# One fused product for q, k and v, one exponential for both heads, and biases carried in shifted weights

## The reference, cut to what matters

```python
ln  = layernorm(layernorm(x)) * g + b          # 4 x 512 x 128
xn  = layernorm(ctx) * g2 + b2                 # 4 x 77 x 96
q   = ln @ Wq.T
k,v = split(concat([xn @ Wkv.T, ln @ Wlkv.T])) # 77 + 512 keys
qn, kn = rmsnorm(q) * scale, rmsnorm(k)        # per head, 2 heads of 64
attn = softmax(where(mask, qn @ kn.T, -max))
x   = x + (attn @ v) @ Wo.T + bo
y   = layernorm(x)
g   = softmax(y @ Wg + bg); top 2 of 8 experts
x   = x + sum over the two of g[e] * (y @ W[e] + b[e])
```

## Time and profile before

| what | us |
|---|---|
| median of 3 timed runs | 128.02 (126.82 to 130.88) |
| span of the profiled execution, first to last instruction | 123.7 |
| median less span (launch and end, and the difference between executions) | 4.3 |
| busy: PE / DVE / POOL / ACT | 106.9 / 97.5 / 91.0 / 76.6 |

### The profile page before, as it was taken

How to read it: one execution, slowest core, us unless ns; L and a number is a source line. 1 busy time by engine, 2 the same in 40 slices (tenths; PEclk the granted TensorE clock), 3 DMA queues, 4 the chain that set the end, 5 groups by cost and what they waited for, 6 DMA issues and landing times. The chain is left out here.

```text
span 123.7 us, 2493 instructions
## 1 busy us (share of the span) xinstructions
PE 106.9 (86%) x683; PEld 69.0 (56%) x683; DVE 97.5 (79%) x376; ACT 76.6 (62%) x177; POOL 91.0 (74%) x117
## 2 busy tenths in 40 slices
PE   0579969999999999999999899999999998589800
PEld 0366957565844763358535356464678885357500
DVE  0746899699598295766988999999899979599780
ACT  1444748784668781985846646797549484843730
POOL 5544699977985789974877191276979998868893
PEclk9999985999999999999999999999999999976995
DMA  4514540000000000000000000000010011101111
GB/s 122 119 22 130 168 169 0 5 0 0 0 3 0 5 0 0 0 0 5 0 5 0 0 0 5 0 0 5 0 42 3 3 42 42 38 10 42 42 42 42
DMA packets 5971, 3.44 MB, mean 28 GB/s; under 512 B 2407, under 2 KB 5575, under 8 KB 5959
## 3 DMA queue, kind: packets, MB, share of 16 engines
q1 hardware_dynamic: 5127, 2.93, 8.0%
q10 hardware_dynamic: 832, 0.36, 1.1%
HBM read 2.24 MB, written 1.05 MB: 27 GB/s over the span
## 5 line engine op out<-in xcount | busy, mean ns | idle before, releaser
L588 ACT ACTIVATE probs<-PS,shift,rk 128x512 f32<-128x512 f32 (+1 forms) x40 | 25.5, 691 | 9.6 <-PE PS L1077 9.3
L635 ACT ACTIVATE scaled<-PS,w 128x128 f32<-128x128 f32 x64 | 18.4, 375 | 9.7 <-PE PS L947 7.0
L1098 PE MATMUL PS<-probs,V_sb 128*64 128x512 f32 (+1 forms) x80 | 18.2, 532 | 0.0
L420 POOL TENSOR_TENSOR esum<-probs,probs 128x1024 f32<-128x1024 f32 (+1 forms) x5 | 10.7, 2147 | 7.2 <-ACT probs L588 7.2
L945 PE MATMUL PS<-WeH,l2H 128*128 128x512 f32 x32 | 14.3, 446 | 0.5 <-ACT scaled L635 0.5
L470 POOL TENSOR_TENSOR pair<-scaled 128x256 f32<-128x256 f32 x16 | 12.0, 751 | 2.8 <-ACT scaled L635 1.5
L946 PE MATMUL PS<-WeL,l2H 128*128 128x512 f32 x32 | 13.3, 414 | 0.0
L947 PE MATMUL PS<-WeH,l2L 128*128 128x512 f32 x32 | 13.1, 410 | 0.0
L429 POOL TENSOR_TENSOR e<-probs,probs 128x1024 f32<-128x1024 f32 (+1 forms) x5 | 9.7, 1936 | 2.6 <-ACT probs L588 2.6
L1077 PE MATMUL PS<-QH,KH 64*128 64x512 f32 (+1 forms) x40 | 9.5, 463 | 0.4 <-DVE QL L766 0.4
L719 DVE TENSOR_SCALAR xh<-x_sb,mv,rstd 128x128 f32<-128x128 f32 x16 | 8.1, 566 | 2.0 <-POOL rstd L388 2.0
(11 more groups left out here) (149 smaller groups left out, 271.3 us busy)
## 6 DMA issues: line engine op xcount, KB each, us to landing
out_dram<-x2b SPq DMA_DIRECT2D x7, 128.0 KB, 1.7
x_sb<-in_x_dram SPq DMA_DIRECT2D x3, 256.0 KB, 3.4
We_sb<-in_L_ffn_W_dram SPq DMA_DIRECT2D x1, 512.0 KB, 5.2
x_sb<-in_x_dram SPq DMA_DIRECT2D x2, 128.0 KB, 2.4
bias_raw<-in_L_ffn_b_dram SPq DMA_DIRECT2D x12, 4.0 KB
Wlkv_sb<-in_L_xattn_Wlkv_dram ACTq DMA_DIRECT2D x1, 128.0 KB, 2.8
out_dram<-x2b SPq DMA_DIRECT2D x2, 64.0 KB, 1.6
ctx_sb<-in_ctx_dram SPq DMA_DIRECT2D x1, 115.5 KB
```

The lines of the kernel that those rows point to most:

```text
L420: pool.tensor_tensor(esum[p % 2][:, :, s], probs[p % 2][0][:, :, s], probs[p % 2][1][:, :, s], ALU.add).then_inc(e01_made, 1)
L588: act.activation(probs[p % 2][n][:, h, s], ps[:, s], ACT.Exp, bias=shift[:, 0:1], scale=rk[:, b, n, h:h + 1]).then_inc(probs_made, 1)
L635: last = act.activation(scaled[m % 2][:, e], ps[:, e], ACT.Copy, scale=w[:, m, e:e + 1])
L1098: last = pe.matmul(bank("value", p, 0)[h * D:(h + 1) * D, s], v, pr, start=(n == 0), stop=(n == KT - 1))
```

## The change

- FRONT has eight units of two tiles, REAR four whole batches. The tables are written anew, and waits count jobs by their place in them.
- `qkv`: one product of 384 columns for a token tile, tokens on the partitions for q, k and v. k goes q's way: one square, one reduce, one power (`rq`, now 8 columns for two tiles), one multiplication (`qkn`), four transposes for two tiles (`qkT`), a split of both. `ssk`, `msk` and `rk` are gone, and the ctx keys go the same way (`ckv`, `ckn`, `ckT`).
- `exp`: one instruction for both heads (two banks, 1024 columns), no scale from a tile, and scores of a tile end in one semaphore.
- `den`: three sources are multiplied by ones and accumulated (e01, e23, ctx), instead of DVE's two additions.
- The layernorm's last channel is replaced by 1, the last row of Wg and of the expert weights by the bias, and that row is subtracted from the others first (the channels of a layernorm sum to zero). `w3`, `gateT`, `wT`, `bias`, `x2b` and the addition of bg are gone; the subtraction (`weS`) and the rest WeL are made on POOL, WeH on ACT.
- The gate is three rounded products of 16 columns for a tile; only l2H is evicted by ACT, and l2L is made by DVE from PSUM.
- `pair`, `low` and `res` take two tiles at once, one store for each pair of tiles.

```diff
 CHOSEN = 3e38
 
 
-FRONT = ((0, 0, 2), (0, 2, 4), (1, 0, 4), (2, 0, 4), (3, 0, 4))
-REAR = ((0, 0, 4), (1, 0, 4), (2, 0, 4), (3, 0, 2), (3, 2, 4))
-
+FRONT = tuple((b, a, a + 2) for b in range(4) for a in (0, 2))
+REAR = ((0, 0, 4), (1, 0, 4), (2, 0, 4), (3, 0, 4))
+JOINED = (0, 1, 2, 3)
 
...
+            sp.dma_start(x_sb[:, 1], xv[1]).then_inc(x_in[1], 16)
             sp.dma_start(gq_b[:], row(qng).to_broadcast([P, D])).then_inc(gains_in, 16)
             sp.dma_start(gk_b[:], row(kng).to_broadcast([P, D])).then_inc(gains_in, 16)
-            sp.dma_start(x_sb[:, 1], xv[1]).then_inc(x_in[1], 16)
             sp.dma_start(mask8[:], mask).then_inc(mask_in, 16)
-            sp.dma_start(bo_b[:], row(bo).to_broadcast([P, C])).then_inc(bias_in, 16)
-            sp.dma_start(bg_b[:], row(bg).to_broadcast([P, E])).then_inc(bias_in, 16)
-            sp.dma_start(Wg_sb[:], Wg).then_inc(Wg_in, 16)
-            sp.dma_start(We_sb[:], We.rearrange("e h o -> h e o")).then_inc(We_in, 16)
-            sp.wait_ge(blk_zeroed, 1)
-            for t in range(T):
-                for k in range(3):
-                    r = k * T * E + E * t
-                    sp.dma_start(bias_raw[r:r + E, t], be).then_inc(blk_in, 16)
             for b in range(2, B):
                 sp.dma_start(x_sb[:, b], xv[b]).then_inc(x_in[b], 16)
+            sp.dma_start(bo_b[:], row(bo).to_broadcast([P, C])).then_inc(bo_in, 16)
+            sp.dma_start(Wg_sb[:], Wg[0:P - 1]).then_inc(Wg_in, 16)
+            sp.dma_start(Wg_last[:], Wg[P - 1:P].to_broadcast([P - 1, E])).then_inc(Wg_in, 16)
+            sp.wait_ge(Wg_zeroed, 2)
+            sp.dma_start(WgS[P - 1:P, 0:E], row(bg)).then_inc(bg_in, 16)
+            sp.dma_start(We_sb[0:P - 1], We[:, 0:P - 1].rearrange("e h o -> h e o")).then_inc(We_in, 16)
+            sp.dma_start(We_last[:], We[:, P - 1:P].rearrange("e h o -> h e o").to_broadcast([P - 1, E, C])).then_inc(We_in, 16)
+            sp.dma_start(We_sb[P - 1:P], be.rearrange("(a e) o -> a e o", a=1)).then_inc(We_in, 16)
 
...
                 step(pool.tensor_scalar(msq[:, b, a:e], ssq[:, b, a:e], 1.0 / D, RMS_EPS * RMS_EPS, ALU.mult, ALU.max))
-                pool.tensor_tensor(rq[:, b, a:e], msq[:, b, a:e],
...
-                pool.tensor_tensor(rk[:, b, a:e], msk[:, b, a:e],
-                                   half[:, 0:H * (e - a)].rearrange("p (t h) -> p t h", h=H), ALU.pow).then_inc(rk_made, 1)
+                pool.tensor_tensor(rqk[:, b, a:e], msq[:, b, a:e],
+                                   half[:, 0:2 * H * (e - a)].rearrange("p (t h) -> p t h", h=2 * H), ALU.pow).then_inc(rqk_made, 1)
...
+            def weS_(p, n):
+
+                pool.wait_ge(We_in, 48)
+                pool.tensor_tensor(We_sb[0:P - 1], We_sb[0:P - 1], We_last[:], ALU.subtract).then_inc(WeS_made, 1)
+
+            def weL_(p, n):
+
+                pool.wait_ge(WeH_made, 1)
+                pool.tensor_tensor(WeL[:], We_sb[:], WeH[:].bitcast(F32), ALU.subtract).then_inc(WeL_made, 1)
...
+            def sq_(p, n):
+                b, a, e = FRONT[p]
+                act.wait_ge(qkv_done, after("pe", "qkv", p))
+                if p >= 2:
+                    act.wait_ge(ssq_made, after("dve", "ssq", p - 2))
+                act.activation(qksq[:, p % 2], both("qkv", p, 0)[:, :, 0:2 * C], ACT.Square).then_inc(qksq_made, 1)
...
+                act.activation(QH[:, b % 2, a * P:e * P], bank("qkT", p, 0)[:, 0:(e - a) * P], ACT.Copy, scale=gain[:, 0:1])
+                act.copy(KH[:, b % 2, a * P:e * P], bank("qkT", p, 0)[:, (e - a) * P:2 * (e - a) * P]).then_inc(qkH_made, 1)
...
+            def weH_(p, n):
+                act.wait_ge(WeS_made, 1)
+                act.wait_ge(We_in, 48)
+                act.copy(WeH[:], We_sb[:]).then_inc(WeH_made, 1)
...
+                ps = both("score", p, n)
                 if n < T:
-                    act.wait_ge(rk_made, through(FRONT, b, n + 1))
+                    act.activation(probs[p % 2][n][:], ps[:], ACT.Exp, bias=shift[:, 0:1], scale=1.0).then_inc(probs_made, 1)
...
-            def ctx_ms_(p, n):
-                dve.wait_ge(css_done, 1)
-                dve.tensor_scalar(cms[:], bank("ctx_ss", 0, 0)[0:M, 0:B * H].rearrange("m (b h) -> m b h", h=H),
-                                  1.0 / D, RMS_EPS * RMS_EPS, ALU.mult, ALU.max).then_inc(cms_made, 1)
-
-            def esum1_(p, n):
-
-                s = slice(0, (REAR[p][2] - REAR[p][1]) * P)
-                dve.wait_ge(e01_made, p + 1)
-                dve.wait_ge(e23_made, p + 1)
-                step(dve.tensor_tensor(esum[p % 2][:, :, s], esum[p % 2][:, :, s], e23[:, :, s], ALU.add))
-
-            def esum2_(p, n):
-
-                s = slice(0, (REAR[p][2] - REAR[p][1]) * P)
-                dve.wait_ge(dve_step, count[0])
-                dve.wait_ge(probs_made, H * KT * (p + 1))
-                dve.tensor_tensor(esum[p % 2][0:M, :, s], esum[p % 2][0:M, :, s], probs[p % 2][T][0:M, :, s],
-                                  ALU.add).then_inc(esum_made, 1)
+            def ctx_ss_(p, n):
...
-            def w3_(p, n):
-
-                b, a, e = REAR[p]
-                s = slice(b * T + a, b * T + e)
...
-                dve.tensor_copy(w3[:, 0, 0:e - a], w[:, s])
-                dve.wait_ge(dve_step, step(dve.tensor_copy(w3[:, 2, 0:e - a], w[:, s])))
-                dve.tensor_tensor(w3[:, 1, 0:e - a], w[:, s], w3[:, 2, 0:e - a].bitcast(F32),
-                                  ALU.subtract).then_inc(w3_made, 1)
-
-            def wT_(p, n):
-                dve.wait_ge(gateT_done, p + 1)
-                if p >= 1:
-                    dve.wait_ge(bias_done, p)
-                dve.tensor_copy(wT[0:3 * T * E], bank("gateT", p, 0)[0:3 * T * E, 0:P]).then_inc(wT_made, 1)
-
-            def x2b_(p, n):
-
-                b, a, e = REAR[p]
-                dve.wait_ge(bias_done, p + 1)
-                dve.tensor_tensor(x2b[:, b, a:e].rearrange("p t c -> p (t c)"), bank("bias", p, 0)[:, 0:(e - a) * C],
-                                  x2[:, b, a:e].rearrange("p t c -> p (t c)"), ALU.add).then_inc(x2b_made, 1)
...
-            def ssk_(p, n):
-                b, a, e = FRONT[p]
-                free("ssk", p, 0)
-                pe.wait_ge(k_made, p + 1)
-                pe.wait_ge(consts_made, 2)
-                for t in range(a, e):
-                    last = pe.matmul(bank("ssk", p, 0)[:, (t - a) * H:(t - a + 1) * H], ksq[:, b % 2, t * P:(t + 1) * P],
-                                     heads[:], start=True, stop=True)
...
+                    last = pe.matmul(both("qkv", p, 0)[:, t - a, 0:3 * C], lnT[:, b % 2, t * P:(t + 1) * P], WT[:],
+                                     start=True, stop=True)
+                last.then_inc(qkv_done, 1)
...
+                for s in range(2):
+                    for t in range(a, e):
+                        k = s * (e - a) + t - a
+                        last = pe.transpose(bank("qkT", p, 0)[:, k * P:(k + 1) * P], qkn[:, p % 2, t - a, s * C:(s + 1) * C], ident[:])
+                last.then_inc(qkT_done, 1)
```

More of the change, by code:

```diff
@@ L241, in bank @@
+        pair = sb("pair", [P, 2, EH // 2, C])
+        low = [sb(f"low{n}", [P, 2, C]) for n in range(2)]
+        acc = [sb(f"acc{n}", [P, 2, C]) for n in range(2)]
+        part = [sb(f"part{n}", [P, 2, C]) for n in range(EH - 1)]
+        PS = [st.enter_context(nc.psum_tensor(f"PS{n}", [P, 2, S], F32)) for n in range(4)]
         def bank(kind, p, n, k=0):
-            return PS[banks[kind, p, n][k]]
+            number = banks[kind, p, n][k]
+            return PS[number // 2][:, number % 2]
@@ L641, in _ @@
+            for kind, p, n in JOBS["act"]:
+                does[kind](p, n)
         @block.vector
@@ L817, in x2_ @@
+                dve.wait_ge(denT_done, after("pe", "denT", b))
+                c = T // 2
+                sums = bank("denT", b, 0)[:, 0:c * P].rearrange("p (c h g k) -> p c h g k", c=c, h=H, g=2)
+                for g in range(a // c, e // c):
+                    divided = step(dve.reciprocal(rden[:, b, g * c:(g + 1) * c], sums[:, :, :, g, 0]))
+                dve.wait_ge(proj_done, after("pe", "proj", p))
                 dve.wait_ge(dve_step, divided)
@@ new lines, in sum_ @@
+                        if e < EH - 1:
+                            summed[i] = step(last)
+                last.then_inc(acc_made, 1)
+            does = dict(consts=consts_, gain=gain_, shift=shift_, mask=mask_, cbias=cbias_, wgsplit=wgsplit_, stats1=stats1_,
+                        apply1=apply1_, ssq=ssq_, qkn=qkn_, qkL=qkL_, ctx_stats=ctx_stats_, ctx_apply=ctx_apply_, ctx_ss=ctx_ss_,
+                        ckn=ckn_, ckL=ckL_, x2=x2_, stats2=stats2_, apply2=apply2_, l2L=l2L_, logits=logits_, mark=mark_,
+                        top=top_, sum=sum_)
@@ L935, in _ @@
+            for kind, p, n in JOBS["dve"]:
+                does[kind](p, n)
         @block.tensor
@@ L1180, in _ @@
```

(10 more changed lines are left out.)

893 lines of the change are left out of this document (390 added, 503 removed).

## The result

The changed kernel takes **159.83 us** (159.06 to 160.62, four runs), the kernel before 128.06 beside it: a ratio of 1.257, 95% interval 1.245 to 1.269. The prediction said 124.2, and its range ended at 129.0. The sign was wrong.

A forecast was written before the change was run, and what follows sets the result against it. PE was taken to set the pace to about 86 us, DVE and POOL to lead the 37.0 us end. 86.6 + 1.5 + 0.6 = 88.7, plus 31.2 gives 119.9 span, plus 4.3 gives 124.2 us; range 119.5 to 129.0.

The forecast's parts named there:

- The step that failed: Middle: the expert-weight subtraction and splits on POOL and ACT are covered; weights wait behind blanks, near 26 us; no cost.
- The slower rival: Later batches: powers in POOL's queue make PE wait 2.3 us before first scores of batches 1-3; 7 us, 131; chance 0.12.
- The front: Start up to the first score: keys now wait for the power, so first score at 20.0 in place of 17.5.
- The chain over the power: Front: batch 1 of x at 10.0, DVE statistics, POOL's two powers to 16.9, then unit 1's remaining steps to 20.0.
- The slow scores: After the first score: the same low-clock stretch again, 2.5 us later, at the same price of 0.43 a pass.
- The middle: First scores to batch 3's last value product: PE sets the pace, elementwise work stays covered; end at 88.7 against 86.6.
- Lag: At 24 us, PE is behind the kernel before by 1.5 us because of the later first score; between 0 and 3.
- PE's work: Removed and added PE jobs nearly cancel: +0.6 us, between -2 and +2; PE gains nothing.
- The paired banks: Middle: scores wait for one long exponential to free both banks, 0.2 each over 20 scores; 4 us, 128; chance 0.15.
- The end: After the last value product: DVE leads, 31.2 us in place of 37.0, saving 5.8.
- the held instructions: End: DVE's last-batch normalisation held once beside POOL's pairs, adding 3.6 us, giving 127.8; chance 0.08.
- From span to time: Whole kernel: median time kept 4.3 us above the profiled span, turning a span of 119.9 into 124.2.

The follow-up runs named there:

- e1_split: Changed kernel with its two large expert-weight loads each cut into loads of 112 and 15 partitions: 122.57 us, ratio to before 0.979.
- h1_122: As e1_split, but with the two loads cut at 122 partitions (122 and 5) in place of 112: 135.58 us, ratio 1.076.
- e4_before_127: Kernel before, with its one expert-weight load over 128 partitions written as loads of 127 and 1: 146.74 us, one run.
- e3_weS_late: Changed kernel with weS moved later in POOL's order and weH later in ScalarE's, loads unchanged: 140.35 us, one run.
- g1_pairs_wait: e1_split with POOL's batch 3 bias addition moved ahead of batch 1's power, and POOL's first batch 1 pair waiting for DVE's last normalisation: 120.41 us.

## Why the prediction was wrong, point by point

**The step that failed** is in the middle: "WeS, WeL and WeH go to POOL and ACT and are covered by the same work", with the expert weights "behind POOL's `blanks`" and "wanted by the first expert product". It looked at the subtractions and let the loads pass unpriced. Two things were left out. The load was not the old one: 128 partitions at 5.2 us from issue to landing had become two loads of 127 at 22 GB/s, 46 us (shown by e1_split, h1_122 and e4_before_127). They were issued at 31.5, too, and not near 26. And it is not the first expert product that wants the weights first: `weS` stands ahead of additions and powers in POOL's order, some 30 us sooner (e3_weS_late). For 35 us of standing and 2 at the lower clock the forecast had zero. I had asked of each engine's instruction what hides it, and of the DMAs only where they are issued. The slower rival, too, looked for a POOL queue that delays PE, but for its powers' length, not for a transfer in it.

**The rest of the sum** can be read off e1_split, whose stages are (front to the first score, middle to the last value product, end), and g1_pairs_wait's end:

```profile
0.00:19.80 19.80, 13.03 (x48) 7.58 (x48) 12.88 (x55) 8.78 (x20) 11.33 (x22) 1.00 0.30 84
19.80:86.90 67.10, 65.76 (x436) 33.25 (x440) 46.48 (x162) 39.14 (x63) 47.65 (x45) 1.00 0.08 17
86.90:120.40 33.50, 25.46 (x152) 19.46 (x152) 28.95 (x122) 18.77 (x67) 23.14 (x26) 0.97 0.10 32
```

```profile
87.10:118.70 31.60, 25.27 (x152) 19.53 (x152) 26.36 (x118) 18.77 (x67) 23.03 (x26) 0.95 0.10 34
```

- The front: first score at 19.80, forecast 20.0. The chain over the power came out, with two small errors against each other: batch 1 was there at 9.2 and not 10.0, and the steps behind the second power (done at 16.5, forecast 16.9) took 3.3 and not 2.9. But the chain did not hold PE alone: the ctx products, 1.9 us from 17.87 that no term of the forecast has there, end at 19.76, and PE goes from them to the score without a pause.
- The slow scores: forecast "the same stretch again". They did not come. From the first score on a pass of both heads takes 0.23 us at clock 1.00, where before it took 0.43. The kernel before had the lower level from 17.8 to 21.2, with PE busy throughout; 3.4 us at half the clock are 1.7 us too many, an estimate from these rows. Why the clock stays up in the new front was not tried.
- The middle: last value product done at 86.9, forecast 88.7. Lag and PE's work together came to +0.2 and not +2.1; by the estimate above most of that is the clock. Of the single prices, `den` of 24 instructions takes 1.44 (forecast 1.5 to 1.7) and a gate of twelve 1.3 (1.3).
- The paired banks: PE idles 1.34 us in the whole middle, and all of it ahead of one `denT` at 63.8, none ahead of a score (e1_split's trace). That rival is out; one exponential of both heads takes 1.11 (taken at 1.2).
- The end: 33.5, forecast 31.2. The missing 2.3 are the held instructions, the rival that I gave 0.08: 2.5 us on the four normalisations of batch 3. With them cured the end is 31.6. The same lies behind the long row of the first normalisation, and could be read in the trace of before: that instruction, the first of the four in DVE's row, starts at 23.05 and lasts 3.97 us, to 27.02; the second of two POOL instructions beside it is over at 26.93.

```profile
23.05 4.74 DVE L719 TENSOR_SCALAR xh<-x_sb,mv,rstd 128x128 f32<-128x128 f32 x4 [1.18 <-POOL rstd L388]
```

```profile
22.98 1.63 POOL L411 TENSOR_TENSOR crk<-cms,half 77x8 f32<-77x8 f32 x1
24.58 2.35 POOL L420 TENSOR_TENSOR esum<-probs,probs 128x1024 f32<-128x1024 f32 x1
```

- From span to time: 4.3 assumed. The profiled execution of e1_split has 122.14 for a span of 120.4, of the changed kernel 159.1 for 157.3: 1.8. The kernel before has 1.8 as well where both numbers are known (126.54 for 124.7, beside g1_pairs_wait). The distance had mixed a fast profiled execution with the median of others; with 1.8 the forecast span of 119.9 would have given 121.7.

So for the kernel without the slow loads the forecast span of 119.9 stands against 120.4: the middle's -1.8 and the end's +2.3 nearly cancel, which is luck and makes that sum look better than its terms.

## What to carry to other kernels

Ask of every load that a change touches into how many equal parts its partitions divide: one row more or less can turn a load of 5 us into one of 23, and here a cut into 112 and 15 mends it. Ask of every instruction that waits for a load not when its result is wanted, but what else is queued behind it and who wants that. And where a cheap elementwise instruction takes three times its usual time, look at what the neighbour engine does at that moment; a wait in the right place on the neighbour made it disappear.

## What was unexpected in the hardware

- Load rate by partition count: 127 partitions 22 GB/s, 122 partitions 44, and cut at 112 up to 204 in a slice, for the same rows of 512 bytes. A broadcast of one row to all partitions was no slower than a load of different rows (22.5 and 23.9 us).
- The issue right behind such a load stands until the load is nearly through: 22.4 to 24.4 us, even where it is a load of one partition (e4_before_127), and everything further back waits, whatever it is for. It shows small, too: behind the gate's weights, 4 KB over the same 127 partitions, the next issue took 2.55 us (changed kernel, at 10.06), where the one behind 128 partitions took 0.43 before.
- DVE's normalisations, copies and products of two SBUF tensors were held to the end of POOL's additions: 1.31 us for 0.34, 0.67 for 0.16, 1.08 for 0.19; statistics and reduces were not. The Trainium skill (GPSIMD Engine Reference, Key points) names such contention for two SBUF inputs and a two-port mode. These rows show how long it lasts: each held instruction ends within 0.1 us of POOL's, whatever its own length.
